# A modulated-convolution and linear kernel: three convolution stages as one 7-tap convolution per sample, and the small tiles of a phase in one run

## What is computed

```
for i, typ in enumerate(('same', 'upsample', 'same', 'downsample')):
    s = style @ mod_w[i].T + mod_b[i]
    weight = SCALE * weights[i] * s[:, None, :, None]
    weight = weight * rsqrt(sum(weight * weight, axis=(2, 3)) + EPS)[:, :, None, None]
    # same: conv, 3 taps; upsample: transposed conv of stride 2, then blur [1,3,3,1]
    # downsample: blur [1,3,3,1], then conv of stride 2; each with a bias
```

## Time and profile before

| | us |
|---|---|
| median of 3 runs | 1305.25 |
| lowest and highest | 1304.34, 1309.24 |
| the profiled execution: time | 1306.01 |
| its span in the trace | 1304.2 |
| PE busy / DVE / ACT / POOL | 1233.0 / 496.3 / 356.1 / 546.2 |
| share of PE in the chain that ended last | 87% |

### The profile page before, as it was taken

One profiled execution on the slowest core, in us unless ns is written; L12 is line 12 of the kernel. 1 busy time (PEld: TensorE's weight loads), 2 busy tenths in 40 slices (PEclk: granted clock), 3 DMA queues, 4 the chain that ended last, 5 costly groups with the idle time before them and its releaser, 6 DMA issues.

```text
span 1304.2 us, 45847 instructions
## 1 busy us (share of the span) xinstructions
PE 1233.0 (95%) x21400; PEld 704.6 (54%) x21400; DVE 496.3 (38%) x975; ACT 356.1 (27%) x757; POOL 546.2 (42%) x417
## 2 busy tenths in 40 slices
PE   5847999999999999999999999999999999999997
PEld 5323556555555555565565555565565554665555
DVE  5612324344333333434333333434333434433343
ACT  2213313223322222313223222312323222312321
POOL 3156641444443442644323543644413544634400
PEclk9968999999999999999999999999999999999999
DMA  8232300002221200000301300000211200000101
GB/s 285 114 105 101 115 17 2 2 3 59 98 105 62 99 3 2 3 2 25 134 27 42 131 3 2 2 2 13 103 53 58 99 3 2 2 2 3 67 2 65
DMA packets 20828, 65.66 MB, mean 50 GB/s; under 512 B 4032, under 2 KB 4416, under 8 KB 16160
## 3 DMA queue, kind: packets, MB, share of 16 engines
q1 hardware_dynamic: 18960, 60.85, 12.8%
q10 hardware_dynamic: 1680, 1.89, 0.5%
HBM read 43.85 MB, written 18.87 MB: 48 GB/s over the span
## 4 chain that ended last, share of the span: by engine, by line
PE 87%; DVE 4%; POOL 1%; issue 1%; ACT 0%; DMA 0%; DVEq 0%; POOLq 0%
PE bank_b L1137 26%; PE bank_a L1068 13%; PE bank_a L1052 11%; PE bank_b L1052 11%; PE bank_b L1003 8%; PE bank_b L1095 5%; PE bank_a L1078 5%; PE bank_a L1027 3%; PE bank_b L1149 2%; PE bank_b L1118 1%; DVE w_sum L957 1%; PE bank_b L1130 1%; POOL xs L716 1%; POOL sum_v L698 1%; DVE z L939 1%
## 5 line engine op out<-in xcount | busy, mean ns | idle before, releaser
L698 POOL TENSOR_TENSOR sum_v<-raw_v 128x768 f32<-128x768 f32 x32 | 58.9, 1842 | 626.5 <-ACT raw_v L760 626.5
L1137 PE MATMUL bank_b<-w_hi,y3t_hi 128*128 128x512 f32 x512 | 210.0, 410 | 12.4 <-DVE w_sum L957 12.1
L1137 PE MATMUL bank_b<-w_hi,y3t_lo 128*128 128x512 f32 x512 | 203.0, 396 | 2.2 <-issue 2.2
L1137 PE MATMUL bank_b<-w_lo,y3t_hi 128*128 128x512 f32 x512 | 202.4, 395 | 0.1
L1068 PE MATMUL bank_a<-y,w_down 64*32 64x512 f32 x3072 | 173.6, 594 | 1.5 <-ACT wv L762 1.5
L1052 PE MATMUL bank_a<-y,wv 32*64 32x512 f32 (+2 forms) x3584 | 145.8, 480 | 2.3 <-issue 2.3
L1052 PE MATMUL bank_b<-y,wv 32*64 32x512 f32 (+2 forms) x3584 | 142.3, 480 | 1.8 <-ACT y L741 1.8
L895 DVE TENSOR_TENSOR x<-bank_b,x 128x512 f32<-128x512 f32 x96 | 66.4, 692 | 202.2 <-PE bank_b L1137 166.0
L753 ACT ACTIVATE y<-bank_a,cb,tab 128x512 f32<-128x512 f32 x64 | 49.7, 776 | 319.4 <-PE bank_a L1068 319.4
L1003 PE MATMUL bank_b<-xs,cw 32*32 32x512 f32 x3072 | 112.0, 615 | 15.3 <-POOL xs L716 15.3
L1137 PEld LDWEIGHTS bank_b<-w_hi,y3t_hi 128*128 128x128 f32 x512 | 96.8, 189 | 50.9 <-DVE w_sum L957 15.6
(11 more groups left out here) (172 smaller groups left out, 1553.0 us busy)
## 6 DMA issues: line engine op xcount, KB each, us to landing
w_hi<-w_scratch SPq DMA_DIRECT2D x9, 1024.0 KB, 5.8
w_lo<-w_scratch SPq DMA_DIRECT2D x9, 1024.0 KB, 8.0
x_in<-in_x SPq DMA_DIRECT2D x32, 256.0 KB, 4.1
out_x<-out_tile SPq DMA_DIRECT2D x32, 256.0 KB, 2.4
w_raw<-w_scratch SPq DMA_DIRECT2D x3, 1024.0 KB, 9.8
w_scratch<-w_hi SPq DMA_DIRECT2D x3, 1024.0 KB, 3.9
w_scratch<-w_lo SPq DMA_DIRECT2D x3, 1024.0 KB, 6.9
w<-in_w SPq DMA_DIRECT2D x2, 1024.0 KB, 13.5
```

The lines of the kernel that those rows point to most:

```text
L698: ins = g_.tensor_tensor(dst[:, :, at:at + count].rearrange("p r k o -> p r (k o)"), src[:, :, 0:count].rearrange("p r k o -> p r (k o)"), ...
L1137: ins = pe.matmul(lin_ps[b][:], y3t[yi][:, k, P * b:P * (b + 1)], w[use(m) % 2][wi][:, k], start=(k == 0 and i == 0), stop=(k == KB - 1 an ...
```

## The change

- `conv2` and `down`, and with them `evacuate_2`, y2 and the ends of y2, are gone. In their place stands `conv(m)`: one convolution of 7 taps for each sample, each tap of 16 matmuls on 32 x 32 tiles with 512 columns, and 6 steps of one column for the ends (`END_STEPS`). 416 records.
- The weights of that convolution are made by TensorE in two products. `products_raw` has 3 steps of 16 matmuls with 128, 96 and 128 columns (96 records). ACT and DVE copy it out as `wr`, 224 columns a bank, with the scale. `products_all` multiplies `wr` with a table of downsampling blocks in 7 steps with 288, 224, 224, 192, 192, 96 and 96 columns (224 records), and ACT and DVE copy 416 columns a bank out as `wv`. `blurred` on POOL is gone.
- The order in an iteration is now `conv(m)`, `products_all(n)`, `conv0(n)`, `products_raw(n + 1)`, all on 32 x 32 tiles, and then `turn(m)` and the linear part of m on the full array. The linear part follows the transposes directly, and nothing else stands between its bases.
- `base(m, 0)` goes through the high parts first and waits for each of them by itself (`y3t_hi`), then through the low parts. `adapter(m)` waits for all low parts, as before. All four `adapted` stand after `base(m, 3)`.
- `effective(m)` and the adapter's results go to `bank_a`, in one piece, and `effective` no longer shares banks with the bases.
- On POOL `scaled_weights(n + 1)` stands right behind `xs`. The end values are added to y3 by DVE (`ends`), four small columns a phase as before.
- The setup has more small matmuls (80 in place of 24 for the first bias product, and a second bias product of 176), a longer chain of small operations on DVE, and `pe.wait_ge(bias_2_ready, 1)` ahead of the matmuls of L463 in place of the wait for ACT's copy.

The diff, cut to its core:

```diff
@@ -39,18 +39,25 @@
+RAW = 2 * TAPS + 1
+RAW_STEPS = ((0, 0, 0, TAPS + 1), (1, 2, 1, TAPS), (2, 3, 1, TAPS + 1))
+
+REACH = TAPS
+ALL, MID = 2 * REACH + 7, REACH + 3
+PAD = REACH
+
+ALL_STEPS = ((3, 2, 9, 9), (1, 5, 2, 7), (5, 1, 0, 7), (2, 5, 20, 6), (4, 2, 18, 6), (6, 10, 26, 3), (0, 0, 29, 3))
+DN = 32
+
+END_STEPS = ((0, LEN - 1, LEN - 2), (1, LEN - 2, LEN - 1), (2, LEN - 1, LEN - 1), (10, 0, 0), (11, 1, 0), (12, 0, 1))
...
+            def bias_out(l, kind, rows):
+                at = (l % 2 * BIASES + kind) * GROUPS * ROWS
+                return ps[l // 2][rows, at:at + GROUPS * ROWS]
+            pe.wait_ge(bias_w_ready, 1)
+            pe.wait_ge(bias_1_ready, 1)
             for l in range(LAYERS):
-                for kind in range(3):
+                for kind in range(BIASES):
+                    for r in range(ROWS):
+                        rows = slice(CH * r, CH * (r + 1))
+                        last = pe.matmul(bias_out(l, kind, rows), bias_w[rows, l, kind], bias_1[rows, l],
+                                         start=True, stop=True)
+            last.then_inc(bias_2_done, 1)
...
-            pe.wait_ge(bias_copied, 2)
+            pe.wait_ge(bias_2_ready, 1)
...
+
+            pe.wait_ge(w0_copied, KB)
+            pe.wait_ge(down_ready, 1)
+            bias_3 = ((("all", 0, 0),), (("all", 1, 0), (2, 0, 1), (3, 0, 2)), ((0, 0, 1), (1, 0, 2)),
+                      ((4, 0, 3), (5, 0, 4)), (("all", 2, 0), (2, 0, 3), (3, 0, 4)))
+            for l in range(LAYERS):
+                for kind, terms in enumerate(bias_3):
+                    for i, (tap, which, of) in enumerate(terms):
+                        for r in range(ROWS):
+                            rows = slice(CH * r, CH * (r + 1))
+                            weights = bias_dn[rows, l, which] if tap == "all" else w_dn[rows, l, 1 + tap]
+                            last = pe.matmul(bias_out(l, kind, rows), weights, bias_2[rows, l, of],
+                                             start=(i == 0), stop=(i == len(terms) - 1), skip_group_check=True)
+            last.then_inc(bias_3_done, 1)
...
-            def blurred(n):
-
-                pool.wait_ge(raw_ready, tiles(n, ROWS))
-                chain_ = ((raw_v, sum_v[0], 1), (sum_v[0], sum_v[1], 1), (sum_v[1], wv, 0))
-                for i, (src, dst, at) in enumerate(chain_):
-                    if i:
-                        pool.wait_ge(v_sums, 2 * n + i)
-                    count = RAW + 1 + i
-                    ins = g_.tensor_tensor(dst[:, :, at:at + count].rearrange("p r k o -> p r (k o)"),
-                                           src[:, :, 0:count].rearrange("p r k o -> p r (k o)"),
-                                           src[:, :, 1:count + 1].rearrange("p r k o -> p r (k o)"), ALU.add)
-                    ins.then_inc(v_sums if i < 2 else wv_ready, 1)
-
             pool.wait_ge(halos_zero, 1)
...
                     nc.gpsimd.tensor_tensor(xs[:, b, 1:LEN + 1], src[:, b], column(n, T_S, b).broadcast_to((P, LEN)),
                                             ALU.mult).then_inc(xs_ready, 1)
+                if n + 1 < PHASES:
+                    scaled_weights(n + 1)
...
-            products(0)
+            products_raw(0)
             for n in range(PHASES + 1):
                 m, convolve, linear = n - 1, n < PHASES, n > 0
+                if linear:
+                    evacuate_3(m)
                 if convolve:
+                    products_all(n)
                     evacuate_0(n)
+                if n + 1 < PHASES:
+                    products_raw(n + 1)
                 if linear:
                     turned(m)
-                if convolve:
-                    evacuate_2(n, 0)
-                    evacuate_2(n, 1)
-                if linear:
                     adapter(m)
                     exponentials(m)
-                if n + 1 < PHASES:
-                    products(n + 1)
-                if linear:
                     adapter_turned(m)
                 if n in MADE_IN:
                     weights_hi(MADE_IN[n])
-                if convolve:
-                    evacuate_3(n)
         @block.vector
...
+            def products_raw(n):
+
+                pe.wait_ge(w2s_ready, n + 1)
+                if n:
+                    pe.wait_ge(wv_act, evacuated(n - 1))
+                    pe.wait_ge(wv_dve, evacuated(n - 1))
+                for i, (tap, at, first, count) in enumerate(RAW_STEPS):
+                            ins = pe.matmul(bank_b[r][CH * c:CH * (c + 1), CH * at:CH * (at + count)],
+                                            w2s[rows, (r + c) % ROWS, CH * tap:CH * (tap + 1)],
+                                            keep["up"][rows, layer(n), first:first + count].rearrange("p k o -> p (k o)"),
+                                            start=(i == 0), stop=True, skip_group_check=True)
+                ins.then_inc(raw_done, 1)
+
+            def products_all(n):
+
+                pe.wait_ge(wr_act, evacuated(n))
+                pe.wait_ge(wr_dve, evacuated(n))
                 if n >= 2:
                     pe.wait_ge(x_ready, tiles(n - 2, ROWS))
+                for i, (block_, at, first, count) in enumerate(ALL_STEPS):
                     for d in range(ROWS):
+                            rows, b = slice(CH * r, CH * (r + 1)), (r + d) % ROWS
+                            ins = pe.matmul(bank_b[r][CH * b:CH * (b + 1), CH * at:CH * (at + count)],
+                                            wr[rows, (b - r) % ROWS, block_],
+                                            keep["down"][rows, layer(n), first:first + count]
+                                            .rearrange("p k o -> p (k o)"),
+                                            start=(i == 0), stop=True, skip_group_check=True)
+                ins.then_inc(all_done, 1)
+
+            def conv(n):
+
+                pe.wait_ge(y0_act, evacuated(n))
+                pe.wait_ge(y0_dve, evacuated(n))
+                pe.wait_ge(wv_act, evacuated(n))
+                pe.wait_ge(wv_dve, evacuated(n))
+                if n:
                     pe.wait_ge(y3t_ready, tiles(n - 1, KB))
-                banks = (bank_b, bank_a)[u]
+                    if (n - 1) % STEP in EFF:
+                        pe.wait_ge(w_sum_ready, summed(n - 1) + KB)
+                steps = [(MID + shift, PAD + shift, LEN, 0) for shift in range(-REACH, REACH + 1)]
+
+                steps[1:1] = [(block_, PAD + col, 1, to) for block_, col, to in END_STEPS]
+                for i, (block_, start, length, to) in enumerate(steps):
+                    for d in range(ROWS):
                         for r in range(ROWS):
+                            rows, a = slice(CH * r, CH * (r + 1)), (r + d) % ROWS
+                            ins = pe.matmul(bank_a[r][CH * a:CH * (a + 1), to:to + length],
+                                            wv[rows, (r - a) % ROWS, block_], y0[rows, a, start:start + length],
+                                            start=(i == 0), stop=(i == len(steps) - 1), skip_group_check=True)
+                ins.then_inc(cv_done, 1)
+                pe.wait_ge(y3_ends, 2 * (m + 1))
                 for k in range(KB):
+                    if m + 1 < PHASES:
+                        evacuation, count = ((y0_act, y0_dve)[k % 2], evacuated(m + 1, k // 2 + 1))
+                        pe.wait_ge(evacuation, count)
                     for b in range(ROWS):
...
-            def effective(m, half):
+            def effective(m):
+                pe.wait_ge(y3t_ready, tiles(m, KB))
+                for k in range(KB):
+                    pe.matmul(bank_a[k][:], keep["a2s"][:, g, P * k:P * (k + 1)], keep["b2s"][:, g],
                               start=True, stop=True).then_inc(eff_done, 1)
...
+                tokens = slice(P * b, P * (b + 1))
+
+                    if b == 0:
+                        pe.wait_ge(y3t_hi, tiles(m, k + 1))
+                    for wi in range(2):
+                        pe.matmul(lin_ps[b][:], y3t[0][:, k, tokens], w[use(m) % 2][wi][:, k],
+                                  start=(k == 0 and wi == 0), stop=False)
+                for k in range(KB):
+                    if b == 0:
+                        pe.wait_ge(y3t_ready, tiles(m, k + 1))
+                    ins = pe.matmul(lin_ps[b][:], y3t[1][:, k, tokens], w[use(m) % 2][0][:, k],
+                                    start=False, stop=(k == KB - 1 and l in (0, 2)))
                 if l in (0, 2):
...
-            def linear_back(m):
+            def linear_plain(m):
+                weights(m)
+                base(m, 0)
+                effective(m)
+                for b in range(1, ROWS):
+                    base(m, b)
+
+            def linear_adapted(m):
+                adapter(m)
+                weights(m)
+                base(m, 0)
+                to_tokens(m)
+                base(m, 1)
+                base(m, 2)
                 adapter_turn(m)
-                base(m, 2)
```

(61 more changed lines are left out.)

447 lines of the change are left out of this document (184 added, 263 removed).

## The result

The changed kernel takes **1479.3 us** (median of 4 runs, 1476.9 to 1482.2) against 1304.8 for the kernel before: ratio 1.133, 95% interval 1.1297 to 1.1363. The forecast was 1258, faster. The profiled execution of the changed kernel took 1478.2 us, its span is 1476.4.

What follows compares the result with a forecast made beforehand. TensorE's stream, busy 95% of the span, plus its few waits was taken as the bound. From 1304.2: -46 -11 -12 +30 -23 +11 +3 = 1256 us span, 1258 us in all; range 1205 to 1290 with rival A.

Steps and rivals of the forecast that it cites:

- the blocks that go and come: Each phase: 15.85 us of conv2, down and products replaced by 14.40 us of small-tile steps, 46 us less in 32 phases.
- Rival B: Instruction stream runs dry in small-tile blocks: one 1.35 us stop a phase gives 1301, two 1344; 5 in 100 each.
- rival A: conv's seven taps overlap better and reach 0.885 us a step: 50 us less, 1208; 14 in 100.
- y3t: Linear part directly after the transposes: new wait of 2.0 us in adapter phases, 30 us more for the 15 newly affected.
- w_sum: PE's eight waits for w_sum disappear because effective moves to bank_a and no base waits for it: 12 us less.
- Start: Start of the main program: no wait for xs and less low clock, 29 us of waits falling to about 6: 23 us less.
- Setup: Setup before the first product: bias_2_ready behind DVE's table, 6.9 us, and 176 small matmuls, 4 us: 11 us more.
- Ends: Six one-column end steps in conv: 1.42 us a phase, upper end 2.27.
- Taps: Seven 512-column taps of conv: 1.11 us a step, 7.77 us a phase, with 0.885 a step as lower end.
- Rival C: Floor of 28 ns for each small matmul record: 247 us more, 1505; 2 in 100.
- Changes of shape: Tile-shape changes fall from seven to two an iteration; three of the five count, at 0.11 us each: 11 us less.
- the end of the program: After the last base, the four adapter results wait two by two for their stores: 3 us more.

Runs made afterwards that it cites:

- e2_spread_ends: Changed kernel with the six end steps of conv placed one behind each of the first six taps instead of all behind the first: 1462.3 us, ratio 1.1217.
- b3_both: Kernel before, with xs of phase 0 ahead of the blurring, and effective's first half ahead of products and base 1 in phases without adapter: 1283.8 us, ratio 0.9834.
- b1_xs_first: Kernel before, with GpSimd making xs of phase 0 before it blurs the products of phase 0: 1298.1 us, ratio 0.9951.
- e1_no_ends: Changed kernel without the six one-column end steps of conv, 384 instructions a phase fewer: 1318.8 us, ratio 1.0121.
- The trains: Kernel before, with trains of 32x32-tile matmuls behind its last phase: 51.5, 26.1, 26.3, 28.2 us for 1, 64, 128, 256 columns; 17.14 us for 16 taps of 512.

## Why the prediction was wrong

**The step that failed** is the one on the blocks that go and come: it priced 16-tile steps by a fixed cost and a cost for each column and let them follow each other at that rate. The rate is there (each block at its shortest in the changed kernel: `conv` 9.67 us, `products_all` 4.22, `conv0` 2.57, `products_raw` 1.89, together 18.4 against my 17.7; no single run has them all, the shortest takes 20.3), but it asks for 1664 instructions in 18 us, 10.9 ns each, and the supply gives one in 13.6 (3.47 us for 256). The phases before had their 1152 small-tile instructions in 19.2 us, 16.7 ns each, with full-array work between. By my prices the blocks at their own rate are worth 46 us less; what they do together costs 218 more than that.

**Rival B was the right mechanism, with the wrong price.** It took the two stops in `products` for accidents of 1.35 us and asked how many there would be. With one stop a phase it had 43 us and with two 86, where the run costs 218, and it gave them 10 in 100 together. Part of the clue was in the trace of before: 168 packets for 168 blocks of 256, and eight stops at one place of a block. But those eight were mostly not the rate. Three stand 3.2 to 3.6 us after the last such place; the other five, the two in `products` among them, stand 5.9 to 7.0 us after it, and their packets had started 3.5 to 4.6 us after the block's begin. A stop at a fixed place says that blocks must arrive; what the new order asks for must then be compared with the rate at which they can. At 6.5 blocks of 3.47 us a phase that gives 22.6 us a run, 4.9 over my 17.7, so 157 us, 1415: slower. For the remaining 60 us or so the trace after has the candidates: the 11 late packets came 34 us later than the usual 1.1 us, in all; 37 of the 103 packets took over 1.2 us instead of 1.0 (14 us in all); and there is the low clock behind the stops. The arrangement of the ends is worth 15 us (e2_spread_ends). These shares overlap, and how they divide was not measured.

**The rest of the steps**, by the trace after:
- y3t: 31.8 us, 16 waits of 2.0; forecast 2.0 in 16 phases. Right.
- `w_sum`: the wait is gone, and b3_both gives 15 us, give or take 4, for its 12. Right.
- Start: the waits for `xs` are gone, 15.3 us, as forecast. But the 23 us did not come. The same work as in the 82.5 us of before, up to the end of the second `conv`, takes from 85.82 to 158.60, 72.8 us; by the prices it is 49.8 instead of 53.2. So waits, stops and low clock still are 23 us, where there were 29: 6 us less, as much as b1_xs_first shows. Of the 23, 8.7 us are in the two `conv`, which take 15.1 and 12.0 us instead of 9.2, with stops and low clock.
- Setup: the first product comes at 85.82 instead of 69.70, 16.1 later, forecast 11. L498 starts at 41.78, as worked out (41.7); the other 5 us are two stops of "issue" in L519's 352 thin matmul records, 5.2 us, both at the same place of a block: the same cause once more.
- Ends: 1.42 us priced; the 192 records run in 1.8, inside the range. `products_all` 3.89 priced, 4.2 at its shortest.
- Taps: 1.11 priced, 1.07 in a long train, but 6.69 us for the seven of e1_no_ends, 0.96 each. The price came from `conv0`, whose three taps start 0.88 us apart with 1.57 us from the last start to the next block; taps from the third on start 1.04 apart. So rival A had about two thirds of its 50 us right, 1.08 us a phase or 35 us, which the supply hid.
- Rival C, a floor of 28 ns for each matmul record: the first block of the one-column train, 128 matmul records, went by in 1.07 us, 8.4 ns each. Out.
- Changes of shape (11 us) and the end of the program (3 us): not measured by themselves.

The Trainium skill's sentence that the refill is hidden (the section named above) speaks of an issue floor of about 20 cycles an instruction. The trains contradict it for TensorE: the first full block of 256 in the train of one column went by in 1.07 us, 4.2 ns an instruction, a third of the 13.6 ns at which they come.

## What to carry to other kernels

Count TensorE's instructions in every dense stretch, weight loads and both passes of fp32 included: where a stretch asked for more than 256 in 3.5 us beyond the first block, the instruction supply set its time, and long full-array matmuls were worth most between the thin ones. Gathering all small matmuls in one run removed changes of tile shape at 0.1 us each and cost 6.8 us a run. In a thin stretch it is also worth looking at the DMA share: the longest stops lay where bulk loads kept the DMA engines busy. And a stop without a cause in the profile is to be looked at for its place before it is priced by its number.

## What the runs showed of the hardware

- TensorE's instructions arrive 256 at a time, one block in 3.47 to 3.49 us in 19 of the 28 steady blocks at 1, 64 and 128 columns (the others 3.0 to 4.0), with one block in reserve after a long stretch of few instructions. The Trainium skill (Runtime: NRT & Kernel Launch, Instruction fetch mechanics) gives TensorE room for 2048 instructions. No run here shows such a reserve: the train of 4096 stops for the first time after some 500.
- The 3.47 us are a round trip: about 1.1 us from PE's begin of a block to the start of the next 16 KB packet, 1.0 for the packet, 1.4 from its landing to the first instruction. Why some packets take 1.3 to 1.4 us or start late with the DMA engines otherwise idle stays open. Beside bulk loads packets started up to 5.6 us after the begin.
- The low clock came with thin records: 0.55 in the train of 1 column (PE busy 22.0 of 52.7 us), 0.64 with 64 (15.0 of 27.0), 1.00 with 128 (15.1 of 26.5), where the stops were just as frequent.
- Columns can be free: the ends at 96 columns cost nothing against the spread ends of one column (ratios 1.119 and 1.1217), at nearly the same clock (0.972 and 0.965).
